# The maxima of the last cross-attention: 590 key columns as two parts of 296, one per bank, read by one operation per block of queries

## The reference

```python
q = lat @ Wq + bq
kv_in = jnp.concatenate([x, lat], axis=1)
kv = kv_in @ Wkv + bkv
k, v = jnp.split(kv, 2, axis=-1)
...
sim = jnp.einsum('bhid,bhjd->bhij', q * scale, k)
sim = sim - jax.lax.stop_gradient(jnp.max(sim, axis=-1, keepdims=True))
attn = jax.nn.softmax(sim, axis=-1)
out = jnp.einsum('bhij,bhjd->bhid', attn, v)
...
return out @ Wout + bout
```

## Time and profile before

| | us |
|---|---|
| median of 3 runs | 1188.86 |
| lowest, highest | 1175.42, 1189.67 |
| profiled execution, its time | 1190.02 |
| profiled execution, span | 1188.3 |

### The profile page before, as it was taken

One profiled execution on the slowest core, in us unless ns is written; L12 is line 12 of the kernel. 1 busy time (PEld: TensorE's weight loads), 2 busy tenths in 40 slices (PEclk: granted clock), 3 DMA queues, 4 the chain that ended last, 5 costly groups with the idle time before them and its releaser, 6 DMA issues.

```text
span 1188.3 us, 18015 instructions
## 1 busy us (share of the span) xinstructions
PE 1091.5 (92%) x6794; PEld 916.1 (77%) x6794; DVE 738.3 (62%) x1733; ACT 608.6 (51%) x1128; POOL 153.0 (13%) x115
## 2 busy tenths in 40 slices
PE   6779999999997468999999999999999999999896
PEld 3558778888886346888889888889888898889532
DVE  5854776556565776666665766665666657663246
ACT  5235543332335436565664656664566656664353
POOL 6110220026625232000000000000000000000001
PEclk9956878999998667999999999999999999999998
DMA  6100000000001000000000000000000000000001
GB/s 221 6 1 1 1 1 1 1 1 1 1 1 36 1 0 1 2 1 2 2 1 2 2 1 2 2 1 2 2 1 2 1 1 2 1 1 2 1 0 36
DMA packets 15680, 10.11 MB, mean 9 GB/s; under 512 B 8759, under 2 KB 14827, under 8 KB 15083
## 3 DMA queue, kind: packets, MB, share of 16 engines
q1 hardware_dynamic: 15595, 8.96, 2.6%
HBM read 7.60 MB, written 1.05 MB: 7 GB/s over the span
## 4 chain that ended last, share of the span: by engine, by line
PE 71%; ACT 15%; DVE 8%; issue 5%; POOL 1%; DMA 0%; POOLq 0%; ACTq 0%; DVEq 0%
PE PS L1399 66%; ACT KA L855 9%; ACT BIG L872 4%; PE PS L1411 4%; PE PS L1761 1%; DVE st L912 1%; DVE X_ODD L923 1%; DVE BIG L1006 0%; DVE mx L1003 0%; DVE X_EVEN L923 0%; DVE mv L915 0%; DVE mxm L1284 0%; ACT BIG L673 0%; ACT BIG L665 0%; DVE VXA L1251 0%
## 5 line engine op out<-in xcount | busy, mean ns | idle before, releaser
L1399 PEld LDWEIGHTS PS<-VXA,BIG 128*128 128x128 f32 (+1 forms) x3136 | 395.9, 191 | 48.1 <-ACT BIG L872 24.5
L1399 PE MATMUL PS<-VXA,BIG 128*128 128x65 f32 (+2 forms) x3136 | 398.4, 272 | 9.4 <-ACT BIG L872 9.4
L872 ACT ACTIVATE BIG<-PS 128x512 f32<-128x512 f32 (+1 forms) x320 | 187.3, 595 | 177.3 <-PE PS L1399 174.4
L1284 DVE TENSOR_REDUCE mxm<-PS 128x1 f32<-128x512 f32 x256 | 170.7, 688 | 96.4 <-PE PS L1399 92.1
L855 ACT ACTIVATE KA<-PS,b1s 64x512 fp32r<-64x512 f32 (+1 forms) x256 | 128.7, 503 | 52.1 <-PE PS L1399 46.4
L1399 PE MATMUL PS<-QA,KA 128*128 128x512 f32 (+1 forms) x320 | 145.1, 453 | 0.0
L548 POOL TENSOR_TENSOR rs<-ve,half_neg 128x4 f32<-128x4 f32 (+1 forms) x29 | 30.1, 1038 | 882.4 <-DVE ve L917 882.4
L1399 PE MATMUL PS<-QB,KB 128*128 128x512 f32 (+1 forms) x320 | 125.6, 393 | 0.0
L1399 PE MATMUL PS<-KA,QA 128*128 128x512 f32 (+1 forms) x512 | 115.8, 329 | 1.8 <-DVE mxm L1284 1.6
L1399 PEld LDWEIGHTS PS<-KA,QA 128*128 128x128 f32 x512 | 86.8, 190 | 21.7 <-DVE mxm L1284 3.6
L777 ACT ACTIVATE BIG<-PS 128x512 f32<-128x512 f32 x72 | 42.7, 599 | 95.7 <-PE PS L1399 95.4
(11 more groups left out here) (249 smaller groups left out, 1584.1 us busy)
## 6 DMA issues: line engine op xcount, KB each, us to landing
X_EVEN<-in_x SPq DMA_DIRECT2D x4, 256.0 KB, 3.9
VXA<-in_L_ffn_Wg SPq DMA_DIRECT2D x1, 1024.0 KB, 5.7
VXA<-in_L_ffn_Wu SPq DMA_DIRECT2D x1, 1024.0 KB, 7.8
VXA<-in_L_ffn_Wd SPq DMA_DIRECT2D x1, 1024.0 KB, 9.5
REG<-in_L_xattn_Wkv SPq DMA_DIRECT2D x1, 1024.0 KB, 4.8
QB<-crow SPq DMA_DIRECT2D x64, 2.0 KB
out<-X_EVEN SPq DMA_DIRECT2D x4, 256.0 KB, 2.3
wq1s<-in_L_xattn_Wq SPq DMA_DIRECT2D x1, 512.0 KB, 8.4
```

The costliest lines, as they stand in the source:

```text
L872: act.activation(PX[0:rows, g % 4, :], PS[0:rows, g % 2, :], ACT.Exp, scale=SCALE_W).then_inc(pw_ready, 1)
L1284: dve.tensor_reduce(mxm[:, p % 2, h, m:m + 1], PS[:, 2 + g % 2, :], AX.X, ALU.max).then_inc(mu_free, 1)
L1399: return pe.matmul(dst, lhsT, rhs, start=start, stop=stop, **kw)
```

## The change

A unit is now one block of 128 queries with all its keys: two matmuls of 296 columns (`MAX_W`), the first over columns 0 to 295 of `KA`, the second over 294 to 589 (two columns are taken twice, which leaves a maximum as it is), into banks 2 and 3. One reduction reads both banks, 2 x 296 elements, and writes two maxima. There are 8 units in a pair in place of 10, and one operation on 8 columns joins the two maxima of all blocks of both heads at the pair's end in place of one on 4 columns per head. Since a unit takes both banks, it waits until the unit just before it was reduced. The units are spread over slots 0 to 5 as 1, 1, 2, 1, 2, 1; before 1, 2, 2, 2, 1, 2.

```diff
+MAX_W = (KEYS_PAD // 2 + 1) // 2 * 2
...
-MAX_UNITS = {0: [0], 1: [1, 2], 2: [3, 4], 3: [5, 6], 4: [7], 5: [8, 9]}
+MAX_UNITS = {0: [0], 1: [1], 2: [2, 3], 3: [4], 4: [5, 6], 5: [7]}
...
-             ("max", 0), ("max", 1), ("norm", 3), ("V", 0, 2), ("max", 2), ("max", 3), ("norm", 4), ("V", 0, 3), ("max", 4),
-             ("max", 5), ("norm", 5), ("latT", 2), ("V", 0, 4), ("max", 6), ("max", 7), ("V", 0, 5), ("max", 8),
-             ("max", 9), ("c", 0), ("Q", 1), ("V", 0, 6), ("K", 1), ("latT", 3), ("V", 0, 7), ("Kt", 1), ("V", 0, 8), ("V", 0, 9)])
+             ("max", 0), ("norm", 3), ("V", 0, 2), ("max", 1), ("max", 2), ("norm", 4), ("V", 0, 3), ("max", 3),
+             ("max", 4), ("norm", 5), ("latT", 2), ("V", 0, 4), ("max", 5), ("max", 6), ("V", 0, 5), ("max", 7),
+             ("c", 0), ("Q", 1), ("V", 0, 6), ("K", 1), ("latT", 3), ("V", 0, 7), ("Kt", 1), ("V", 0, 8), ("V", 0, 9)])
...
-        mxm = sb("mxm", [P, 2, 2, NT])
-        mxt = sb("mxt", [P, 2, 2, NT])
+        mxm = sb("mxm", [P, 2, 2, NT, 2])
...
             def maxima(p, u):
 
-                h, m = divmod(u, 5)
-                g = 10 * p + u
+                g = 2 * NT * p + u
                 dve.wait_ge(mu_full, g + 1)
-                if m < NT:
-                    dve.tensor_reduce(mxm[:, p % 2, h, m:m + 1], PS[:, 2 + g % 2, :], AX.X, ALU.max).then_inc(mu_free, 1)
-                else:
-                    dve.tensor_reduce(mxt[:, p % 2, h, :], PS[:, 2 + g % 2, 0:NT * (KEYS_PAD - S)].rearrange("p (t k) -> p t k", t=NT),
-                                      AX.X, ALU.max).then_inc(mu_free, 1)
+                dve.tensor_reduce(mxm[:, p % 2, u // NT, u % NT, :], PS[:, 2:4, 0:MAX_W], AX.X, ALU.max).then_inc(mu_free, 1)
+                if u == 2 * NT - 1:
                     dve.wait_ge(mu_free, g + 1)
-                    dve.tensor_tensor(cmx[:, p % 2, h, :], mxm[:, p % 2, h, :], mxt[:, p % 2, h, :], ALU.max).then_inc(cm_ready, 1)
+                    dve.tensor_tensor(cmx[:, p % 2], mxm[:, p % 2, :, :, 0], mxm[:, p % 2, :, :, 1], ALU.max).then_inc(cm_ready, 1)
...
             def max_unit(p, u):
-                h, m = divmod(u, 5)
-                g, r = 10 * p + u, p % 3
+                h, t = divmod(u, NT)
+                g, r = 2 * NT * p + u, p % 3
                 if u == 0:
                     pe.wait_ge(hi_ready, 12 * (p + 1))
                     pe.wait_ge(pj_free, PJ["Kt", p] + 1)
-                if g >= 2:
-                    pe.wait_ge(mu_free, g - 1)
-                if m < NT:
-                    mm(PS[:, 2 + g % 2, :], QA[r][h][:, P * m:P * m + P], KA[r][h][:, 0:S]).then_inc(mu_full, 1)
-                else:
-                    w = KEYS_PAD - S
-                    for t in range(NT):
-                        ins = mm(PS[:, 2 + g % 2, w * t:w * t + w], QA[r][h][:, P * t:P * t + P], KA[r][h][:, S:KEYS_PAD])
-                    ins.then_inc(mu_full, 1)
+                if g:
+                    pe.wait_ge(mu_free, g)
+                for i in range(2):
+                    ins = mm(PS[:, 2 + i, 0:MAX_W], QA[r][h][:, P * t:P * t + P], KA[r][h][:, (KEYS_PAD - MAX_W) * i:(KEYS_PAD - MAX_W) * i + MAX_W])
+                ins.then_inc(mu_full, 1)
...
-                    pe.wait_ge(cm_ready, 2 * (p + 1))
+                    pe.wait_ge(cm_ready, p + 1)
```

## The result

The changed kernel takes **1241.7 us** (median of 4 runs, 1236.1 to 1243.7) against 1189.3 for the kernel before on the same chip: ratio **1.049** (95% interval 1.042 to 1.056), 4.9% slower. The forecast was 1240, 4.3% over the median. The profiled execution after has a span of 1241.8 us, before 1188.3: 53.5 us, or 4.5%, to account for.

The account below looks back on a forecast made before the run. TensorE's issues and waits were taken to bound the last cross-attention stage. 45.3 us for pairs 0 to 29, 1.7 for pair 30 and 3 ahead of the stage make +50.0 on 1190.0: 1240 us, range 1224 to 1262.

Parts of the forecast that it names:

- The wait: TensorE, slots 2 and 4: the second of two adjacent units waits for the first's reduction, 1.11 us, two a pair.
- Slots 0 to 3: First part of a pair: nothing covers the first wait, +1.11 less 0.42 of saved columns, +0.69 us.
- Slots 4 to 7: Second part of a pair: TensorE comes 1.05 us later, the old wait absorbs about a quarter, +0.82 us.
- Both: Slots 0 to 3 and 4 to 7 together, 0.69 + 0.82 us more a pair.
- All pairs: Pairs 0 to 29 cost 45.3 us more, and pair 30, without evictions, 1.7.
- Ahead of the stage: Pair 0's own units, side by side three times, leave VectorE idle: +3 us, between +1 and +4.
- VectorE's load: VectorE's work per pair falls from 6.1 to 5.7 us, counted as nothing since its idle third hides it.
- The waits are not shorter: Rival it rejects: waits of 0.95 us or partly hidden, 1218 us; chance 0.08 for 1205 to 1224.
- the columns do not win: Rival it rejects: TensorE's 0.48 us a pair of saved columns decides, giving 1175 us; chance 0.02.
- 296 columns do not cost as 512: Rival it rejects: matmuls of 296 columns cost as much as 512, 45 us more, 1285; chance 0.04.
- VectorE is free at A: Forecast margin 0.1 us in slot 2; the rival, VectorE busy then, gives 1255, up to 1262; chance 0.10.
- The clock's fall: Rival: the granted clock falls in one tenth of the stage, 58 us more, 1298 in all; chance 0.06.

Follow-up runs that it names:

- e12: Kernel before, two 512-column units a pair (slots 1 and 3) made to wait for the unit just before: ratio 1.050.
- e3: Changed kernel with one unit per slot, the two left over computed for the pair after next in slots 8 and 9: ratio 1.003.
- e7: Changed kernel with one unit per slot, the two left over computed for the pair after next in slots 7 and 8: ratio 0.995.
- e8: Changed kernel, one unit per slot, slot 3 empty, last unit in slot 6, and units moved apart ahead of the stage: ratio 0.992.
- e14: Changed kernel, one unit per slot, two in slots 7 and 8 of the pair before, units moved apart ahead of the stage: 1173.4 us, ratio 0.985.
- e9: Kernel before, two units of 78-column matmuls a pair (slots 2 and 5) made to wait for the unit just before: ratio 1.146.
- e1: Kernel before, every unit made to wait for the one just before instead of the last but one: ratio 1.175.
- e2: Changed kernel with pv between the two units of slots 2 and 4, and VectorE's low part between their reductions: ratio 1.020.
- e10: Kernel before, three units a pair (slots 1, 2 and 3) made to wait for the unit just before: ratio 1.096.
- e13: Changed kernel with its second double slot moved from slot 4 to slot 5: ratio 1.041.
- e11: Changed kernel with one reduction per bank, each matmul waiting for its own bank alone: ratio 1.033.

## Why the prediction was right

- **The wait.** Its mechanism and its place are shown: e12 has it, at 1.07 us each, with the old shapes, e3 and e7 have none with the new ones. Ready 0.48 (forecast 0.47), reduction 0.775 (0.77), release 0.05 (0.05), weights 0.12 (0.10), spacing of an undelayed unit 0.27 (0.28): 1.15 instead of 1.11.
- **Slots 0 to 3**: +0.66 (forecast +0.69). **Slots 4 to 7**: +0.86 (+0.82); pv(6) starts 7.18 us behind slot 4's scores (7.14). **Both**: +1.53 (+1.51) a pair. The pairs that make values take 21.3 to 22.0 (21.9).
- **All pairs** from the first scores to the last crow: 1.7 + 46.5 = 48.2 (forecast 45.3 + 1.7 = 47.0); 62 waits of 1.15 instead of 1.11 are 2.5 more, and the saved columns and the old wait in slot 7 take a little of it back.
- **Ahead of the stage**: +4.2 where the sum had +3. This term was mis-sized: it took each of the three waits at 0.8, from 0.62 at full clock and 0.9 at half. All three gaps on VectorE are 0.95, and the clock was 0.50 there instead of the 0.65 of the earlier trace rows. Two of them:

```profile
437.41 0.77 DVE L1282 TENSOR_REDUCE mxm<-PS 128x2 f32<-128x592 f32 x1 [0.95 <-PE PS L1395]
441.44 0.78 DVE L1282 TENSOR_REDUCE mxm<-PS 128x2 f32<-128x592 f32 x1 [0.95 <-PE PS L1395]
```

  Three of 0.95, and 0.3 and 0.5 for two value copies, give 3.7; the 0.5 left is not assigned. e8 and e14, with the units moved apart, take 38.6 and 38.4 us for this stretch, so it is the order of the units that costs. Their clock there is 0.72, though, and how much of the 4.2 is the waits and how much the lower clock is not separated; e7, in the order of the changed kernel at 0.62, took 41.9 instead of 42.9.
- **VectorE's load** fell by 0.18 a pair (12.24 to 12.06), not by 0.4; as it was counted as nothing, the sum did not feel it.
- **Luck in the number.** The profiled execution took 1243.5 us, 3.5 over the forecast. That the median lies only 1.7 over it says little: four executions of the kernel before spread over 24 us.
- **The range's rivals.** The waits are not shorter, the columns do not win, 296 columns do not cost as 512 (0.14 each), VectorE is free at A by 0.09. The clock's fall did not happen in the changed kernel, but e9 and e1 show that it was nearer than a chance of 0.06 says: two waits a pair ahead of 78-column units cost 14.6% instead of 5%. The reason given against it, that a wait of 0.75 leaves the clock at 1.00, was not enough: in e9 waits of 0.78 did not leave it there.

## What to carry to other kernels

Before merging two tiles into one to save instructions, count how many buffers are left: with one, two users in a row must stand apart by ready time, consumer and release (here 0.48 + 0.775 + 0.05 = 1.30 us), and the whole consumer moves onto the producer's path. Putting other work between them (e2) gave back a third, since the next user was not spaced and the consumer's engine had other work queued ahead. Spread the users evenly first, then merge: here that turned 4.9% slower into about 1% faster than before. Read a gain in the stage that the edit touches, since the rest varies by as much from one execution to the next.

## What was unexpected of the hardware

**The same wait, with and without a fall of the clock.** Waits of TensorE of 0.8 to 1.0 us, two in each pair, left the granted clock of the stage at 1.00 with a 512-column unit behind each (e12) or two matmuls of 296 (after), and at 0.84 with four of 78 and eight of 65 behind (e9); three a pair gave 0.98 (e10), one ahead of every adjacent unit 0.89 (e1). The longer waits were not the worse ones: in e9 it fell behind 29 of 31 waits of 0.78 us in slot 5 and behind 14 of 30 of about 1.04 in slot 2. Width and place changed together between e9 and e12, and e13, with two matmuls of 296 behind a wait in slot 5, fell 4 times of 31 in the one execution that was profiled; which of the two decides is not shown.

**One reduction over two banks costs what its elements do.** 592 elements in two banks take 775 ns; the line through 312 (473) and 512 (688) in one bank gives 774. Two separate ones of 296 take 125 ns more, at 1.80/4 = 0.45 us each in e11.
